# Joining the cross attention and the feed-forward of a decoder layer in one block, and regrouping the last scatter

## The reference

```
x = layernorm(x + self_attention(x))          # 32 heads of 16, causal, ALiBi
x = layernorm(x + cross_attention(x, ctx))    # 32 query heads of 128, 8 key heads,
                                              # keys from 512 context rows and the 256 of x, q and k rms-normed
x = layernorm(x + ffn(x))

ffn:  t = x[:, perm]                          # permute the 512 columns
      t = gelu(einsum('bhd,hdm->bhm', t, up)) # 16 heads, 32 -> 128
      t = einsum('bhm,hmd->bhd', t, down)     # 128 -> 32
      return t[:, argsort(perm)]              # permute back
```

## Time and profile before

| | us |
|---|---|
| median of 3 runs | 848.48 (847.68 to 849.51) |
| the profiled execution | 847.78 |
| its span | 846.0 |
| busy in the span: TensorE matmuls | 825.7 (98%) |
| VectorE / ScalarE / GpSimd | 547.8 / 475.4 / 522.1 |
| last head's final unit to the cross attention's last matmul | 782 to 809.7 |
| feed-forward block | 810.1 to 846 |

### The profile page before, as it was taken

The page is one execution under the profiler, slowest core; times in us unless marked ns, Lnnn a source line. Parts: engine busy times, 40 slices in busy tenths (PEclk is TensorE's granted clock), DMA queues, the critical chain, the costliest instruction groups (busy, mean ns, idle before and its releaser), DMA issues. The chain is left out here.

```text
span 846.0 us, 15109 instructions
## 1 busy us (share of the span) xinstructions
PE 825.7 (98%) x4841; PEld 693.0 (82%) x4841; DVE 547.8 (65%) x1505; ACT 475.4 (56%) x1005; POOL 522.1 (62%) x676
## 2 busy tenths in 40 slices
PE   7999999999999999999999999999999999999986
PEld 5777777777788888888888888888888888888764
DVE  4466566765345776667666766677667767777654
ACT  5666665566246565555555555556455645556543
POOL 3577876767336566765766666765775676536741
PEclk9999999999999999999999999999999999999999
DMA  7613223121141721221102101122122102000011
GB/s 226 186 38 117 84 75 109 55 76 51 50 138 54 250 77 38 69 69 39 50 24 86 62 21 68 37 68 68 37 68 68 37 4 76 4 0 1 1 26 50
DMA packets 48510, 56.22 MB, mean 66 GB/s; under 512 B 4670, under 2 KB 29772, under 8 KB 48460
## 3 DMA queue, kind: packets, MB, share of 16 engines
q1 hardware_dynamic: 48460, 55.59, 21.5%
HBM read 41.95 MB, written 13.63 MB: 66 GB/s over the span
## 5 line engine op out<-in xcount | busy, mean ns | idle before, releaser
L1251 POOL TENSOR_SCALAR prob<-prob,x_rinv 128x768 f32<-128x768 f32 x124 | 112.6, 908 | 173.4 <-DVE x_rinv L1425 173.4
L1362 ACT ACTIVATE pT_hi<-bank 128x512 fp32r<-128x512 f32 x192 | 114.3, 598 | 90.1 <-PE bank L1575 90.0
L1345 ACT ACTIVATE prob<-bank,x_nm,q_rms 128x768 f32<-128x768 f32 x124 | 123.3, 995 | 47.2 <-DVE x_nm L1419 46.7
L1465 DVE TENSOR_TENSOR pT_lo<-bank,pT_hi 128x512 fp32r<-128x512 f32 x192 | 130.2, 679 | 5.1 <-ACT pT_hi L1362 3.7
L1416 DVE TENSOR_REDUCE x_mx<-bank 128x1 f32<-128x768 f32 x124 | 118.3, 954 | 22.0 <-PE bank L1529 21.6
L1575 PE MATMUL bank<-ident,prob 128*128 128x128 f32 x768 | 114.8, 272 | 2.1 <-POOL prob L1251 1.3
L1575 PEld LDWEIGHTS bank<-ident,prob 128*128 128x128 f32 x768 | 95.0, 140 | 14.0 <-POOL prob L1251 2.0
L48 PE MATMUL bank<-pT_hi,xv_hi 128*128 128x512 f32 x192 | 86.5, 450 | 1.2 <-DVE pT_lo L1465 0.8
L485 ACT ACTIVATE s_self<-s_self,nm_self 128x128 f32<-128x128 f32 (+1 forms) x128 | 57.1, 448 | 43.1 <-DVE nm_self L628 42.6
L50 PE MATMUL bank<-pT_hi,xv_lo 128*128 128x512 f32 x192 | 75.7, 394 | 0.0
L49 PE MATMUL bank<-pT_lo,xv_hi 128*128 128x512 f32 x192 | 75.4, 393 | 0.0
(11 more groups left out here) (227 smaller groups left out, 2043.1 us busy)
## 6 DMA issues: line engine op xcount, KB each, us to landing
wo_raw<-in_Wo SPq DMA_DIRECT2D x8, 1024.0 KB, 5.4
v_by_head<-v_st SPq DMA_DIRECT2D x12, 512.0 KB, 3.3
kT_by_head<-kT_st SPq DMA_DIRECT2D x12, 512.0 KB, 3.2
xk_raw<-kT_by_head SPq DMA_DIRECT2D x16, 384.0 KB, 3.2
xv_raw<-v_by_head SPq DMA_DIRECT2D x16, 384.0 KB, 3.2
wq_raw<-in_Wq SPq DMA_DIRECT2D x6, 1024.0 KB, 5.5
wq_raw<-in_w_attn SPq DMA_DIRECT2D x12, 256.0 KB, 3.9
xk_raw<-in_ctx SPq DMA_DIRECT2D x8, 256.0 KB, 2.6
```

Source lines behind the costliest of these rows:

```text
L1251: nc.gpsimd.tensor_scalar(prob[:, s, :], prob[:, s, :], rinv[:, s:s + 1], 1.0, ALU.mult, ALU.mult)\
L1345: nc.scalar.activation(prob[:, s, :].rearrange("p (a e) -> p a e", a=2), bank[:, at:at + 2, 0:HALF], ACT.Exp, bias=nm[:, s:s + 1], scale=q ...
L1362: nc.scalar.activation(pT_hi[:, a, :], bank[:, turn.bank[s, what, a], :], ACT.Copy)\
L1465: nc.vector.tensor_tensor(pT_lo[:, a, :], bank[:, turn.bank[s, what, a], :], f32(pT_hi[:, a, :]), ALU.subtract).then_inc(ring_out, 1)
```

## The change

Five things are edited. (1) The feed-forward is called inside the block of the cross attention and takes that stage's buffers; no barrier stands between. Its DMAs for `up` and `down` wait for the last split of the output weights. (2) The index rows and gather matrices are made among the norms of the last head's final unit, the fourth one and the scatter matrices straight behind. (3) All four reciprocal roots of x2 are made in one row after the parts of `up`; the remainders `residual_lo` come when all of x2 is made. VectorE normalises tile 2 before the lo part of tile 1. (4) TensorE transposes tile 2 before the first permute, and the last tile into two banks, in two halves that ScalarE and VectorE take one by one. (5) The scatter goes tile by tile; the last tile is computed in two halves of 256 columns in two banks, with statistics per half.

```diff
@@ GpSimd, last head @@
+            def gather_matrix(i):
+                nc.gpsimd.tensor_scalar(k.gather[:, i, :], perm_row, index_col[:, i:i + 1], None, ALU.is_equal)\
+                    .then_inc(matrix_made, 1)
...
+                else:
+                    permutation()
+                    gather_matrix(0)
                 norms(2, (0,))
...
-                norms(2, (1, 2, 3))
+                    norms(2, (1, 2, 3))
+                else:
+                    gather_matrix(1)
+                    norms(2, (1,))
+                    gather_matrix(2)
+                    norms(2, (2, 3))
...
             turns(pool, body)
+            gather_matrix(3)
             for i in range(KT):
                 nc.gpsimd.tensor_scalar(k.scatter[:, i, :], index_row, perm_cols[:, i:i + 1], None, ALU.is_equal)\
                     .then_inc(matrix_made, 1)
-            for i in range(TT - 1):
-                inverse_deviation(i)
@@ VectorE, end of the last head @@
                     normalise(1)
-                    x2_lo(0)
                     dve.wait_ge(ring_out, turn.end + 1)
                     statistics(2)
+                    x2_lo(0)
+                    normalise(2)
                     x2_lo(1)
@@ feed_forward, buffers @@
+        up, up_hi, up_lo = by_head(wo_raw[:, 0, :]), by_head(k.k_hi[:, 0, 0:D]), by_head(k.k_lo[:, 0, 0:D])
+        tT_hi, tT_lo = k.qT_hi, k.qT_lo
+        hid = [flat[:, HPT * TOK * i:HPT * TOK * (i + 1)].rearrange("p (r t) -> p r t", t=TOK) for i in range(KT - 1)]
+        hid.append(k.wq_raw[:])
+        ident_r = k.k_hi[:, 1, 0:P]
+        res_hi, res_lo = pT_hi[:, 0:TT, :], pT_lo[:, 0:TT, :]
+        yT_hi, yT_lo = wo_hi, wo_lo
-        block = ctx.enter_context(nc.Block())
+        last_z = bank[:, Z_BANK[TT - 1]:Z_BANK[TT - 1] + 2, 0:D // 2]
+        X3_BANK = (3, 0)
@@ SP @@
+            sp.wait_ge(wo_split, PIECE * KVH)
@@ GpSimd, feed-forward: the parts of up first, then @@
+            for i in range(TT):
+                pool.wait_ge(k.var_made, i + 1)
+                nc.gpsimd.tensor_tensor(k.rstd[:, i:i + 1], k.var[:, i:i + 1], k.minus_half[:, 0:1], ALU.pow)\
+                    .then_inc(k.rstd_made, 1)
+            pool.wait_ge(x2_made, TT)
+            for j in range(TT):
+                residual_lo(j)
@@ ScalarE @@
+            for half in range(2):
+                act.wait_ge(x3t_ps, half + 1)
+                chunks, rows = last_chunks(half)
+                nc.scalar.activation(xT_hi[:, chunks, tokens(3)], rows, ACT.Copy).then_inc(x3t_hi, 1)
@@ VectorE, feed-forward @@
-            normalise(2)
+            dve.wait_ge(k.ring_full, k.ring_drained + 1)
             nc.vector.tensor_tensor(x[:, TT - 1, :], bank[:, k.last_bank, :], x[:, TT - 1, :], ALU.add).then_inc(x3_sum, 1)
...
+            last_stats = k.stats[:, 0:2, :]
+            for half in range(2):
+                dve.wait_ge(z_ps, TT + half)
+                nc.vector.bn_stats(last_stats[:, half, :], last_z[:, half, :]).then_inc(y_stats, 1)
+                if half == 0:
+                    make_shift(TT - 2)
@@ TensorE @@
+            pe.wait_ge(k.matrix_made, KT)
+            pe.wait_ge(k.ring_out, k.ring_drained)
             pe.wait_ge(xt_lo, 2)
+            transposes(2)
             permute(free[0], 0)
             permute(free[1], 0)
-            transposes(2)
             permute(free[2], 0)
             transposes(3)
             pe.wait_ge(x3_sum, 1)
             permute(held, 0)
-            pe.wait_ge(xt_lo, TT)
+            pe.wait_ge(xt_lo, TT - 1)
...
-            residual((0, 1))
+            residual(0)
+            residual(1)
             down_products(3)
-            residual((2, 3))
-            scatter_group(0, range(TT))
-            scatter_group(1, range(TT))
-            for js in ((0, 1), (2, 3)):
-                scatter_group(2, js)
-                scatter_group(3, js)
+            residual(2)
+            pe.wait_ge(k.matrix_made, 2 * KT)
+            for j in range(2):
+                for i in range(KT - 1):
+                    scatter_group(i, j)
+            for j in range(2):
+                scatter_group(KT - 1, j)
+            for i in range(KT):
+                scatter_group(i, 2)
+            for half in range(2):
+                residual(TT - 1, half)
+                for i in range(KT):
+                    scatter_group(i, TT - 1, half)
```

More of the change, by code:

```diff
@@ L1648, in feed_forward, with columns, last_chunks @@
         Z_BANK = (2, 3, 5, 6)
-        block = ctx.enter_context(nc.Block())
+        last_z = bank[:, Z_BANK[TT - 1]:Z_BANK[TT - 1] + 2, 0:D // 2]
+        HALF_D = D // 2
+        X3_BANK = (3, 0)
+        def columns(half):
+            return slice(half * HALF_D, (half + 1) * HALF_D)
+        def last_chunks(half):
+            return slice(2 * half, 2 * half + 2), bank[:, X3_BANK[half], 0:2 * P].rearrange("p (k t) -> p k t", k=2)
         def tokens(j):
@@ L1738, in make_shift @@
                                         ALU.mult, ALU.mult).then_inc(shift_made, 1)
-            def normalise(i):
-                nc.vector.tensor_scalar(x[:, i, :], x[:, i, :], k.mv[:, 0, i, 0:1], k.rstd[:, i:i + 1],
-                                        ALU.subtract, ALU.mult).then_inc(x2_made, 1)
-            normalise(2)
+            dve.wait_ge(k.ring_full, k.ring_drained + 1)
             nc.vector.tensor_tensor(x[:, TT - 1, :], bank[:, k.last_bank, :], x[:, TT - 1, :], ALU.add).then_inc(x3_sum, 1)
@@ L1751, in _ @@
             nc.vector.tensor_scalar(k.var[:, TT - 1:TT], k.mv[:, 0, TT - 1, 1:2], LN_EPS, None, ALU.add).then_inc(k.var_made, 1)
-            dve.wait_ge(x3_rstd, 1)
-            normalise(3)
-            for j in (2, 3):
-                dve.wait_ge(xt_hi, j + 1)
-                nc.vector.tensor_tensor(xT_lo[:, :, tokens(j)], bank[:, j, :].rearrange("p (k t) -> p k t", k=KT),
-                                        f32(xT_hi[:, :, tokens(j)]), ALU.subtract).then_inc(xt_lo, 1)
+            dve.wait_ge(xt_hi, 3)
+            nc.vector.tensor_tensor(xT_lo[:, :, tokens(2)], bank[:, 2, :].rearrange("p (k t) -> p k t", k=KT),
+                                    f32(xT_hi[:, :, tokens(2)]), ALU.subtract).then_inc(xt_lo, 1)
+            dve.wait_ge(k.rstd_made, TT)
+            nc.vector.tensor_scalar(x[:, TT - 1, :], x[:, TT - 1, :], k.mv[:, 0, TT - 1, 0:1], k.rstd[:, TT - 1:TT],
+                                    ALU.subtract, ALU.mult).then_inc(x2_made, 1)
+            for half in range(2):
+                dve.wait_ge(x3t_hi, half + 1)
+                chunks, rows = last_chunks(half)
+                nc.vector.tensor_tensor(xT_lo[:, chunks, tokens(3)], rows, f32(xT_hi[:, chunks, tokens(3)]), ALU.subtract)\
+                    .then_inc(x3t_lo, 1)
             def permuted_lo(i):
@@ L1776, in _ @@
                 result_split(i)
-            for i in range(TT):
+            for i in range(TT - 1):
                 statistics(i)
@@ L1788, in transposes @@
                 pe.wait_ge(x2_made, j + 1)
+                if j == TT - 1:
+                    pe.wait_ge(xt_lo, 2)
                 for i in range(KT):
-                    last = nc.tensor.transpose(bank[:, j, tokens(i)], x[:, j, i * P:(i + 1) * P], ident[:])
-                last.then_inc(xt_ps, 1)
+                    if j < TT - 1:
+                        at = bank[:, j, tokens(i)]
+                    else:
+                        at = bank[:, X3_BANK[i // 2], tokens(i % 2)]
+                    last = nc.tensor.transpose(at, x[:, j, i * P:(i + 1) * P], ident[:])
+                    if j == TT - 1 and i % 2:
+                        last.then_inc(x3t_ps, 1)
+                if j < TT - 1:
+                    last.then_inc(xt_ps, 1)
             def permute(i, b):
@@ L1796, in permute @@
                 for j in range(KT):
+                    if b == B - 1 and i == 0 and j % 2 == 0:
+                        pe.wait_ge(x3t_lo, j // 2 + 1)
                     nc.tensor.matmul(bank[:, 4 + i, w], gather[:, j, tokens(i)], xT_hi[:, j, w], start=j == 0, stop=False)
```

114 lines of the change are left out of this document (61 added, 53 removed).

## The result

| | before | changed |
|---|---|---|
| median, timed together | 848.46 (847.68 to 849.51, 6 runs) | 845.58 (844.89 to 845.97, 6 runs) |
| profiled execution | 847.78 | 845.65 |
| span | 846.0 | 843.8 |
| first softmax exponential of the cross attention's query stage | 264.22 | 265.48 |
| from there to the span's end | 581.78 | 578.32 |

The ratio is 0.9964, 95% interval 0.9954 to 0.9975: 3.05 us faster, between 2.1 and 3.9 (the two medians lie 2.88 apart). The forecast was 845.0, 3.5 faster, with a range of 843.6 to 846.9. TensorE's granted clock over the span was 0.999.

The account below looks back on a forecast made before the run. TensorE, busy 98% of the span, was taken as the bound, with gains only in its waits and the tail. Second permutes 2.37 us earlier plus 1.13 at the last norm make 3.5, predicting 845.0 (range 843.6 to 846.9).

Parts of the forecast that it names:

- Matrices among the norms: GpSimd, last head: matrices fit its idle time, TensorE keeps 1.4 us of cover, scatter matrices end at 798.2; no gain counted.
- Roots: Reciprocal roots of x2 on GpSimd: first ready at 803.12, not 804.77; second transposes of x2 0.35 us earlier.
- The lo part of tile 1: VectorE ends it at 809.60; TensorE newly waits for it and starts the transposes of tile 2 at 809.63.
- Normalise 3: VectorE's last x2 normalisation takes 0.55 us instead of 1.50, since GpSimd's residual subtractions wait until x2 is complete.
- Half copies: Tile 3's two half copies on ScalarE and VectorE: about 0.4 us each, no wait; at full cost 0.6 lost.
- Tail: Scatter and last norm: half-width statistics take 0.43 us, last normalisation starts 1.13 us earlier (bounds 0.86 to 1.21).
- B: Rival: matrices stretch VectorE's small x_nm scalings by 1.4 and 0.9 us, giving 847.3; chance 0.04.
- C: Rival: only the opening pays; TensorE's scatter order or two-bank reads eat the scatter's gain, giving 846.1; chance 0.08.
- part 3: Scatter tile by tile with the last tile in halves: last normalisation 1.13 us earlier.
- D: Rival: branches cost VectorE 0.65 and half copies the full width, about 1 us less gain, 846.0; chance 0.08.
- E: Rival: normalisation of tile 3 stays at 1.5 or gelus wait elsewhere, tail bound as before; 848.5, no change; chance 0.06.
- A: Rival: matrices ahead of norms on in-order GpSimd delay the last head, TensorE 4.8 us late, 849.8; chance 0.05.

Follow-up runs that it names:

- Experiment 6: Changed kernel with index rows and all four gather matrices ahead of the last head's four norms; 845.07 us, ratio to before 0.9961.
- experiment 9: Changed kernel with each engine's feed-forward instructions written straight behind its cross attention's, without a branch; 845.59 us, ratio to before 0.9958.
- experiment 4: Changed kernel without GpSimd's wait for all of x2, so residual subtractions run beside VectorE's normalisation of tile 3; 846.01 us, ratio to before 0.9970.
- experiment 2: Changed kernel with the scatter in its old order and last-tile statistics at full width; 846.34 us, ratio to before 0.9974.
- experiment 7: Changed kernel with index rows, four gather and three scatter matrices ahead of the last head's four norms; 849.56 us, ratio to before 1.0015.

## Why the prediction was right

The mechanism and the sum held. Point by point, in the time of before:

- Matrices among the norms: first norm at 782.97 forecast, 782.91 found; TensorE not held (791.85, 791.83); scatter matrices to 798.2, 798.1. Experiment 6 shows that the cover was there even with all four gather matrices ahead of the norms.
- Roots: normalise 1 at 806.23, 806.24 found; second transposes at 807.28, 807.26.
- The lo part of tile 1 ends at 809.60, 809.59 found. But TensorE's transposes of tile 2 start at 809.86 and not 809.63. This term was mis-sized: 0.04 was put for the reaction to a semaphore, it was 0.27; experiment 9 rules the branch out, and what makes it is open. It carries through to the second permutes: 814.60 against 814.36, so 2.13 earlier than before and not 2.37.
- Normalise 3: 0.55 forecast, 0.55 found, and the reason shown by experiment 4: beside GpSimd's first subtraction the normalisation ends at 815.06, 0.29 behind that one's end (813.49 + 1.28), as in the trace of before. The Trainium skill, SBUF — State Buffer, section "Who interferes with whom", says that a VectorE instruction in a two-port mode and a GpSimd instruction block each other fully, the second waiting for the first. The two traces agree with that. They do not exclude a steady slowing, since VectorE begins 0.06 to 0.07 behind GpSimd in both.
- Half copies: 0.66 and 0.76 for two each, so about 0.4 as taken, and no wait.
- Tail: half statistics 0.43 forecast, 0.43 found; last normalisation 1.13 earlier than the rest's shift, 1.16 found (842.61 - (840.58 - 1.26) - 2.13); experiment 2 gives 1.25, the 0.17 behind the last normalisation included.
- Sum: 3.50 forecast, 2.13 + 1.16 + 0.17 = 3.46 found. That the sum comes this close is in part luck, since two errors cancel: 0.24 too much at the hole; 0.17, or 0.1 to 0.2 with the rounding of the spans, too little behind the last normalisation, from which the span's end is 2.38 to 2.45 away in the traces with the new scatter and 2.58 to 2.60 in those with the old one (before and experiment 2). The four stores are issued within 4.32 us in the first and within 3.13 or 3.14 in the second; whether that is the reason no run shows.

Of the rivals, B is refuted by the row of x_nm: two of its last pieces, at 785.27 and 789.03, lie inside matrices (785.06 to 786.63, 788.32 to 789.89), and it takes 214 ns on average as before.

```profile
785.27 0.21 DVE L1423 TENSOR_SCALAR x_nm<-x_mx,q_rms 128x1 f32<-128x1 f32 x1
...
789.03 0.21 DVE L1423 TENSOR_SCALAR x_nm<-x_mx,q_rms 128x1 f32<-128x1 f32 x1
```

```profile
L1423 DVE TENSOR_SCALAR x_nm<-x_mx,q_rms 128x1 f32<-128x1 f32 x124 | 26.6, 214 | 4.4
```

C does not hold (experiment 2: part 3 is worth 1.25). D does not either: without a branch the distance stays at 578.30 (experiment 9), and the two half copies together take 0.66 and 0.76, where a full one takes 0.60 and 0.69, and no permute waits for them. E falls with the normalisation of 0.55 and the early last statistics. A did not come about. Its price was worked out as 4.8 for a fully serial GpSimd; experiment 7 lost 5.0, of which 3.6 are the wait and 1.4 TensorE's clock, the part that was not thought of.

The medians came out at 845.58 and 845.21 where 845.0 stood. The forecast took the 0.7 between before's median and its profiled execution as an offset that stays. But each execution draws its start anew: the first exponential lies between 264.2 and 266.6 in the fourteen traces.

## What to carry to other kernels

An edit worth 0.4% is read from a distance between two marks inside the trace, behind the part of the kernel that varies; traces of one kernel repeated their distance within 0.1 us (578.32 and 578.27; 581.78, 581.79 and 581.82), while the medians of before over 6 to 24 runs lay between 848.08 and 849.12. Work off the critical path on an in-order engine is placed by its readers: here it had 1.4 us of cover and 6.9 us of holes, the same matrices behind the last norm cost 2.7, and three more of them ahead 5.0. Before a barrier is taken out, look at what waits there anyway: the barrier itself was worth 0.3 of the 2.1 gained up to the second permutes, the order around it the rest.

## What the runs showed of the hardware

- The start of a launch varies. TensorE's first projection matmuls run at 0.63 us instead of 0.39 for 6 to 13 instructions, in before and changed kernels alike (8 in the first trace of before, 13 in its second); the granted clock in the first trace of before was 0.50 of full speed from 11 to 13 us, the 1.2 GHz level. In that of the changed kernel, as in eleven of the fourteen traces, the view shows full speed over the stretch while the matmuls take 0.63, so there the durations have to be read. The start of the first of them (9.15 to 10.60, set by when x lands) plus 0.2 for each slow one and a constant 253.5 gives the first exponential within 0.2 in all fourteen traces: 9.15 + 1.6 + 253.5 = 264.25 (264.22), 9.67 + 2.6 + 253.5 = 265.8 (265.91), 10.08 + 1.4 + 253.5 = 265.0 (265.08).
- A GpSimd comparison against a column (`is_equal`, 128x512, L1266) takes 1.57, a multiplication of the same shape (L1700) 0.62 to 0.63.
- VectorE's scalings of one element per partition are not held by GpSimd (124 of them at 214 ns on average, GpSimd busy 62% of the span), while one of 128x512 that begins 0.06 behind a GpSimd subtraction takes 1.51 instead of 0.55 (experiment 4).
